# A two-layer network with two mixtures of experts on one core: the space for the descriptors of indexed DMAs, 2048 or 16384 bytes a partition

## The reference

```
x = x + L0_attn(layernorm(x))   # gated recurrence over time, then a feed-forward part with GELU
x = x + L0_ffn(layernorm(x))    # mixture of 16 experts, 2 chosen for each token, hidden 256, ReLU
x = x + L1_attn(layernorm(x))   # attention, 16 heads of 8, rotary embedding
x = x + L1_ffn(layernorm(x))    # attention, layernorm, mixture of 8 experts (2 a token, hidden 512, GELU), layernorm
```

## Time and profile before

| what | value |
|---|---|
| median of 3 runs | 2563.66 us (2563.43 to 2563.97) |
| the profiled execution | 2584.42 us |
| its span, first to last instruction | 2582.3 us |
| indexed DMAs on POOL | 152 at L550, 165.7 us busy; 128 at L646, 134.7 us busy |
| queue of the indexed DMAs | 8960 packets, 18.37 MB, 2.9% of the 16 DMA engines' span |

### The profile page before, as it was taken

How to read it: one execution, slowest core, us unless ns; L and a number is a source line. 1 busy time by engine, 2 the same in 40 slices (tenths; PEclk the granted TensorE clock), 3 DMA queues, 4 the chain that set the end, 5 groups by cost and what they waited for, 6 DMA issues and landing times. The chain is left out here.

```text
span 2582.3 us, 45707 instructions
## 1 busy us (share of the span) xinstructions
PE 2042.4 (79%) x16904; PEld 968.8 (38%) x16904; DVE 1997.2 (77%) x3408; ACT 1496.1 (58%) x2908; POOL 581.2 (23%) x696
## 2 busy tenths in 40 slices
PE   6889884774359999999999669999999999359910
PEld 5677663763122222222222222222222222359910
DVE  6676677665678999999997488999999995576635
ACT  3434431132124998989989426988989889105510
POOL 2232220365731000000000160000000000316555
PEclk9899895698677999999999879999999999559965
DMA  5000001125261011011010260101111100302211
GB/s 188 1 0 0 0 0 41 35 86 95 75 188 35 19 32 42 19 41 32 24 23 6 65 199 17 32 23 37 33 28 32 35 13 10 120 12 66 66 50 55
DMA packets 94394, 120.94 MB, mean 47 GB/s; under 512 B 23664, under 2 KB 56560, under 8 KB 93936
## 3 DMA queue, kind: packets, MB, share of 16 engines
q1 hardware_dynamic: 73712, 78.92, 11.1%
q0 software_dynamic: 8960, 18.37, 2.9%
q10 hardware_dynamic: 11520, 20.98, 2.6%
HBM read 69.70 MB, written 42.99 MB: 44 GB/s over the span
## 5 line engine op out<-in xcount | busy, mean ns | idle before, releaser
L1349 DVE TENSOR_REDUCE mx<-psum 128x1 f32<-128x1024 f32 x1024 | 1174.9, 1216 | 77.2 <-PE psum L1237 76.2
L1326 ACT ACTIVATE p<-psum 128x512 f32<-128x512 f32 x2048 | 1102.6, 596 | 107.3 <-PE psum L1259 64.9
L1271 PE MATMUL psum<-p,v_ext 128*32 128x256 f32 x8192 | 655.4, 392 | 39.3 <-ACT p L1326 39.2
L1237 PE MATMUL psum<-ks,qs 64*128 64x512 bf16 x2048 | 635.1, 393 | 52.6 <-DVE mx L1349 30.0
L1259 PE MATMUL psum<-qs,ks 64*128 64x512 bf16 x2048 | 630.0, 383 | 1.5 <-ACT p L1326 1.3
L1271 PEld LDWEIGHTS psum<-p,v_ext 128*32 128x32 f32 x8192 | 161.9, 108 | 474.1 <-ACT p L1326 255.2
L1259 PEld LDWEIGHTS psum<-qs,ks 64*128 64x128 bf16 x2048 | 123.4, 93 | 402.9 <-ACT p L1326 367.0
L1139 POOL CAST m_near<-mx 128x16 bf16<-128x16 f32 x128 | 25.3, 198 | 1075.8 <-DVE mx L1349 1071.7
L606 ACT ACTIVATE hid<-psum,stage 128x128 f32<-128x128 f32 x448 | 132.4, 367 | 205.0 <-issue 99.0
L550 POOL DMA_INDIRECT x_in<-n_rows,token_of x152 | 165.7, 1090 | 263.4 <-POOLq L85 173.2
L576 PE MATMUL psum<-x_t,stage 128*128 128x128 f32 x896 | 139.2, 293 | 29.2 <-issue 21.1
(11 more groups left out here) (204 smaller groups left out, 2109.4 us busy)
## 6 DMA issues: line engine op xcount, KB each, us to landing
qs<-qk_parts SPq DMA_DIRECT2D x128, 104.0 KB
ks<-qk_parts SPq DMA_DIRECT2D x128, 104.0 KB
qk_parts<-piece__1 ACTq DMA_DIRECT2D x40, 256.0 KB
qk_parts<-piece__2 ACTq DMA_DIRECT2D x40, 256.0 KB
answers<-y_out SPq DMA_DIRECT2D x152, 64.0 KB
ew<-in_moe SPq DMA_DIRECT2D x1, 5136.0 KB, 18.2
ew<-in_moe SPq DMA_DIRECT2D x1, 4624.0 KB, 14.0
n_rows<-n_all SPq DMA_DIRECT2D x8, 512.0 KB, 3.2
```

The source lines that it names most:

```text
L1237: pe.matmul(psum[:, bank, :], a["qs"][r, g % NKF, j % KM, i * P:(i + 1) * P], a["ks"][r, g % NKF, j % KM, k * HALF:(k + 1) * HALF], start= ...
L1271: last = pe.matmul(psum[GR * j:GR * j + VW, O_BANK, q], t["v_ext"][:, b * NT + i, VE * (h0 + j):VE * (h0 + j) + VW], a["p"][:, (GH * s + j ...
L1326: act.activation(a["p"][:, n % NP, :], psum[:, S_BANK + n % NS, :], ACT.Exp, scale=DH ** -0.5)\
L1349: dve.tensor_reduce(a["mx"][:, g % 2, h, j, 0, c:c + 1], psum[:, bank:bank + 2, :].rearrange("p a c -> p (a c)"), AX.X, ALU.max)\
```

## The change

```
-    nc = bacc.Bacc("TRN2", target_bir_lowering=False, num_devices=1, dynamic_dma_scratch_size=2048)
+    nc = bacc.Bacc("TRN2", target_bir_lowering=False, num_devices=1, dynamic_dma_scratch_size=16384)
```

## The result

The change made the kernel faster by 18.4 us.

| | median us | lowest to highest | the profiled execution | its span |
|---|---|---|---|---|
| 2048 bytes | 2563.30 | 2559.75 to 2563.97 | 2584.42 | 2582.3 |
| 16384 bytes | 2544.91 | 2540.42 to 2547.79 | 2544.78 | 2542.7 |

The account below looks back on a forecast made before the run. The prediction took POOL's pauses between indexed DMAs, read as a full descriptor space, to bound the kernel. 7.60 + 10.25 + 0 + 0 = 17.85 us off 2563.66 gave 2545.8 us, range 2542 to 2557.

Parts of the forecast that it names:

- No pause remains, in either stage: POOL's fetches in `attention_inputs` and the last stage: room for 112 DMAs, at most 80 a stage, so no pauses.
- Term 1: Last stage (`finish`): four pauses of POOL between fetches, 8.80 us less the usual gaps of 1.20, save 7.60 us.
- Term 2: First `attention_inputs`: four pauses of POOL between fetches, 11.45 us less the usual gaps of 1.20, save 10.25 us.
- rival (b): `attention_inputs` gives its gain back to the stores of the pieces; only 7.60 us stay, 2556.1 us; chance 0.14, whole or part.
- Term 3: Gathers of both mixtures (80 and 72): their pauses are covered by POOL running up to 8 tiles ahead; worth 0.
- Term 4: The tensors' new place in SBUF: no effect on access times, taken as 0, within 0.02 us for a 2 us piece.
- Emptied between stages: Descriptor space taken as empty at each stage's start, since both fetch stages pause first at their 15th fetch.
- (a): Rival: DMA count runs through the whole run; two pauses remain, 33rd fetch of `attention_inputs`, 9th of `finish`; 2549.6 us; chance 0.08.
- (c): Rival: pauses come from other bookkeeping of fixed size, such as a limit on DMAs in flight; unchanged, 2563.7 us; chance 0.12.
- (d): Rival: each issue becomes dearer as more unreclaimed DMAs lie in the larger space; slower, 2581.5 us; chance 0.04.
- The slow fetches stay: Last stage: POOL instructions of 2.58 and 1.98 us in place of 0.95, while VectorE mixes and scales, remain.
- POOL waits until everything in flight has landed: Reading of the pauses at fetches: a full descriptor space makes POOL wait for all DMAs in flight, 3.11 us start to start.

Follow-up runs that it names:

- space_1024: The kernel before with the descriptor space cut from 2048 to 1024 bytes, first chip: 2572.76 us, ratio 1.0051 to the kernel before.
- pad_2048: The kernel before, space still 2048 bytes, plus an unused tensor of 14336 bytes a partition ahead of all others, first chip: 2561.69 us, ratio 1.0001.
- same_2048: The kernel before, unchanged at 2048 bytes, run and profiled once more on the first chip: 2561.90 us, ratio 1.0002.
- again_16384: The changed kernel (16384 bytes) run once more, on the second chip: 2583.15 us, ratio 0.9992 to the kernel before on that chip.
- run 2734: Not the label of a run: 2734 counts the VectorE instructions that increment a semaphore over one whole execution.

## Why the prediction was right

The likeliest case came true, in time (2544.91 against 2545.8) and by its steps:
- **No pause remains, in either stage.** Right. The idle time "issue" at L646 came down to 38.1 us, "about 38" was forecast.
- **Term 1, the last stage, 7.60 us.** Measured 7.78. Its length is 86.99 us, forecast 87.2.
- **Term 2, `attention_inputs`, 10.25 us.** From first to last fetch the stretch fell from 101.02 to 90.63 us, by 10.39. Of that, 9.05 are left at the first gather of the second mixture, so up to 1.3 us were given back behind the stretch (in `space_1024` 3.3 of 7.7 were). This is what remains of rival (b); its mechanism, the stores, was not tested by itself. One of my reasons against (b) was misread: of VectorE's waits in the earlier trace rows two are named after ScalarE, none after POOL. The window that corresponds to the earlier trace rows shows the same crowd, only earlier (columns as there):
```profile
712.00:752.00 40.00, 24.46 (x72) 9.89 (x72) 31.65 (x43) 9.93 (x17) 18.48 (x12) 0.71 0.81 239
```
- **Term 3, the gathers, 0.** Measured -1.31 and +0.50, sum -0.8; a stretch in which no indexed DMA runs differs by 1.25 in the same two traces, so 0 stands within what the pair can tell.
- **Term 4, the place, 0.** Right, by `pad_2048`: 1.0001.
- **Emptied between stages.** Not shown. The first pause is at the 15th (or 8th) fetch in both stages, at two sizes and at two places of the tensors, but the semaphores' rule gives that without any emptying, as worked out above. With 112 places the oldest have long landed when the space fills, so the step made no difference to the time.
- **Rivals (a), (c), (d)** fell: no pause anywhere in the 128 fetches, the size does set where the first one stands (8th, 15th), and the fetches' durations don't grow. Of (a) only the two pauses are refuted, not that the count runs on through the stages.
- **The slow fetches stay**, as forecast: 2.58 or 2.59 us at fetches 20, 36 and 52 of the last stage and 1.98 at 25, 41 and 57, before and after. That the trace "agrees" with VectorE holding POOL up is shown for some of its instructions alone: in the profile of before fetches 20 and 25 both end 0.82 us after the end of the line beside which they started (L663, L820), but fetches 19 and 24, beside L659 and L203, took 0.97 and 0.96.

What I had wrong lies in the mechanism, not in the sum. "POOL waits until everything in flight has landed" gives the first pause, but not the spacing of 16, which I had left as unexplained, nor 4096 bytes without a pause. The wait that fits every run is for the newest DMA on the oldest one's semaphore. For 16384 bytes both readings say "no pause", so the forecast could not fail by it; for 4096 it did, by 14 us (2554 expected, 2540.33 measured). Part of my support for "14" was no support: the idle times of the gathers in the earlier trace rows, 1.21, 1.17 and 2.47 us, are named after TensorE there, and they don't come back in `same_2048`, where the idle time is 0.30 or 0.31 us between all gathers of the first mixture and 0.30 before the 15th of the second. They come with the late signals of the profile of before, and with eight semaphores in turn the gathers had no such pause to lose. So term 3 was 0 for another reason than TensorE's lead.

The descriptors' arithmetic that stands on the Trainium skill ("DMA: Bandwidth & Descriptors", the table of terms and "The descriptor swizzle": 16 bytes a descriptor, 8 data descriptors and one for completion) gives, as an estimate from that page's figures, room for 14.2 DMAs in 2048 bytes and 7.1 in 1024. The runs agree: 14 and 7 were found.

The profiled execution was the wrong base for the size of the gap: I took it that its 20.8 us above the median came from profiling. The unchanged kernel profiled again took 2561.14 us, within 1 us of its median. That the sum didn't suffer is luck: the stretch of term 2 has late signals in that profile (last section), but the lengths between fetches came out alike in both, 100.94 and 94.82 us there, 101.02 and 94.77 in `same_2048`. The timed runs, too, were of the kind in which the change helps. On the second chip the same change measured 0.9992, which the forecast would have missed, and nothing in its reasoning tells the two apart.

Open: whether 8 semaphores at 2048 bytes would be as fast as 16384 on the first chip (they ran on the others alone); whether 4096 is really better than 16384 (0.9918 and 0.993 come from different runs and their intervals overlap), which also leaves no version shown to beat the changed kernel; why at 2048 bytes an idle time of 0.93 to 1.31 us, where 0.6 is usual, stands before every seventh gather of the second mixture (22, 29, 36, ... 71), at 4096 before every 21st (29, 50, 71), and at 16384 six of the eight are gone. 7 is 14 less 7 and 21 is 28 less 7, so these may be the places where gathers are given back, all but the last seven at a time; the rule doesn't give that number, and it would be the one sign of the 28 places at 4096 bytes.

## What to carry to other kernels

Unnamed idle time before indexed DMAs that comes at fixed numbers of them can be the descriptor space. Count how many fit (14 of 128 rows in 2048 bytes here), then look at which semaphore each reports to: in these runs the pause comes when the oldest one shares its semaphore with one just issued, and either more space (4096 was enough here) or eight semaphores in turn remove it. That the time follows is shown for the space, on the first chip; for the semaphores only the pauses are. Before a difference between two profiles is explained, compare each profile's own time with the runs: here 23.2 of the 39.6 us were there with no change at all.

## What was not expected of the hardware

- **Two levels of one kernel.** The unchanged kernel takes 2561.35 us on the first chip and 2586.97 and 2589.64 us on the second and third, with the same mean granted clock (0.88). The profile of before is of the slower kind though its timed runs aren't. Each chip was measured in one group of runs, so whether the level belongs to the chip or to something else that differed is not shown.
- **What differs is when semaphore signals arrive.** For each VectorE instruction that increments a semaphore, the time in us from its end to the next recorded increment of that semaphore, from the traces:

```
                    us of the span   median   90th percentile
same_2048, after    480 to 620       0.01     0.01
before              480 to 620       0.01     2.96
before              620 to 730       0.01     11.6
again_16384         2285 to 2440     0.01     15.8
before, again_16384 900 to 1100      0.01     0.01
```

Where signals are late some of their records are missing too (before, 480 to 620: 152 records for 241 increments; none missing in `same_2048`), so the table shows that they are late, and how late only roughly. Over the whole run 2734 instructions of VectorE increment a semaphore. The time is above 0.2 us for none of them in `same_2048` and after, for 198 in before and for 279 in `again_16384`, and all of these stand in the stretches with indexed DMAs (488 to 720 and from 2315 on). What they cost shows in the first gathers. The window of the kernel before, in its own profile (columns as in the earlier trace rows):
```profile
483.00:560.00 77.00, 55.08 (x376) 46.97 (x376) 40.36 (x126) 26.17 (x84) 50.46 (x51) 0.90 0.28 78
```
The same window of `same_2048`, the same program:
```profile
483.00:560.00 77.00, 67.24 (x478) 56.38 (x479) 50.15 (x159) 33.20 (x106) 59.32 (x59) 0.96 0.36 94
```
376 matmuls against 478 in the same 77 us, 51 instructions of POOL against 59. From first gather to first fetch it is 138.01 us against 120.14. Why signals are late on one chip and not on another no run here shows, nor whether it is the DMAs that delay them.
- **A gain that isn't there everywhere.** Where signals are late, the change is worth 0.9992 [0.9981, 1.0003]. Between the profile of before (late signals too) and `again_16384`, 9.6 us are won from first to last fetch of the last stage (94.82 to 85.25), of which 3.3 are lost again behind the last fetch (20.10 to 23.45), and 8.7 are lost from the first fetch of `attention_inputs` to the second mixture (1689.19 to 1697.88): 3.6 of them up to the last fetch, the other 5 behind it, which was not followed up.
